# Scattering the second layer's expert results by choice and token, and joining the weighted sum to the expert stage

## The chip, the cores and the metric

The kernel runs on one core of a Trainium2 chip. The metric is the device time of one execution in microseconds (us). The trace numbers every time from the start of its own span. The engines are TensorE (PE; its weight loads are PEld), VectorE (DVE), ScalarE (ACT), GpSimd (POOL) and SyncE (SP), each with its own queue of instructions; SPq, ACTq and POOLq are the queues' DMA issues.

## What is computed

A decoder of two layers over 2048 tokens of width 256, in float32. Each layer adds an attention and a mixture of experts to the residual x. The change concerns the second layer's experts:

```python
N = T * K                    # 2048 tokens, 4 choices each, 32 experts
C = 2 * N // E               # capacity of an expert: 512 rows
scores = softmax(x @ gate_w.T); topk_w, topk_ids = top_k(scores, K); topk_w /= topk_w.sum(-1)
order = argsort(flat_ids); tok = order // K
pos = arange(N) - starts[sorted_eid]
buf = zeros((E, C, 256)).at[sorted_eid, pos].set(x[tok], mode='drop')
g, u = split(einsum('ech,ehf->ecf', buf, w13)); eo = einsum('eci,eih->ech', silu(g) * u, w2)
out_slots = eo[sorted_eid, pos]          # beyond the capacity this reads the expert's last row
routed = zeros_like(x).at[tok].add(out_slots * flat_w[order][:, None])
out = residual + routed + shared
```

The first layer's experts have no capacity.

## The kernel before, in words

The program is a row of blocks, with all engines meeting between them: `norm_block0`, `route_block` 0, `attention_block0` over batches 0 and 1 ("scatter"), `expert_block` 0, `attention_block0` over batches 2 and 3 ("combine"), `norm_block1`, `route_block` 1, `attention_block1`, `expert_block` 1, `combine_block1`. Each block has one instruction stream for each engine, written by hand, with semaphores between them; `wait_ge` stops the engine that carries it and all that is queued behind.

Routing gives each pair of token and choice a slot in `xs`, a table in device memory of 96 tiles of 128 rows; each expert owns whole tiles. `tile_expert` says which expert a tile belongs to. `xs` is filled with zeros at the start (12 DMAs of 1 MB), then GpSimd scatters the normalised rows of `s.xn` there, one indirect DMA for one token tile and one choice (`scatter_tile`, line 761). In the second layer 24 of these 64 run in `route_block` 1, which begins with the first only when VectorE has written the slots (lines 743 and 744), and 40 in `attention_block1`.

`expert_block` works through 95 tiles. SyncE loads a tile of `xs` into one of four buffers (line 1185). TensorE turns it with two transposes (line 1209), multiplies it with the gate and up weights (line 1219), turns the hidden values (line 1228) and multiplies them with the down weights (line 1237). VectorE copies the turned rows (line 1291), makes the product of gate and up (line 1297) and copies the turned hidden values (line 1303). ScalarE does the silu (line 1264) and copies the result into one of four buffers (line 1271), and issues its store to `ys` (line 1273). In step i TensorE does tile i's two gate/up products with tile i+2's transposes between, then turns tile i-1's hidden values, then multiplies tile i-2's with the down weights (first layer: i-8's).

`combine_block1` follows the barrier. GpSimd gathers the 64 tiles of 128 rows (16 token tiles, 4 choices) from `ys` by slot (line 1708); VectorE adds each to x with its weight (line 1720), four for a tile, each waiting for the one before; SyncE stores two token tiles of x together (line 1701). A pair beyond the capacity has the slot of the expert's last row for this gather and an index out of range for the scatter.

In `attention_block0` ScalarE and GpSimd split the query weights of a head into a high and a low part (lines 1101, 856), SyncE loads `wq` and `khT` for each head (lines 837, 841), and GpSimd also makes the keys and sums the rotated query (lines 867, 872).

## Time and profile before

| | us |
|---|---|
| median of 3 timed runs | 1323.95 (1322.92 to 1324.11) |
| profiled execution | 1324.33 |
| its span in the trace | 1323.1 |
| PE busy | 1102.8 (83%) |
| DVE busy | 780.4 (59%) |
| ACT busy | 522.8 (40%) |
| POOL busy | 510.3 (39%) |

The busy times are sums over the whole span, through stages that have different limits. The mean granted TensorE clock is 0.92 of full speed. DMA moved 167.21 MB.

### The profile page before, as it was taken

How to read it: one execution, taken by the hardware profiler on the slowest of the kernel's cores; microseconds unless marked ns; L12 is line 12 of the kernel's file. 1: busy time of each engine (PE TensorE's matmuls, PEld its weight loads, DVE VectorE, ACT ScalarE, POOL GpSimd, SP SyncE). 2: the span in 40 equal slices, each digit the busy share in tenths (PEclk: the TensorE clock that was granted, in tenths of full speed). 3: DMA queues.
4: the chain of work that ended last, by engine and by line, in shares of the span. 5: the costliest groups of instructions: out<-in, count | busy, mean ns of one | idle time of the engine just before them, and what ended most of it. 6: DMA issues, size and time to landing. Idle time of an engine off the chain costs nothing. (4 is left out here: it accounts for less than half of the span.)

```text
span 1323.1 us, 19843 instructions
## 1 busy us (share of the span) xinstructions
PE 1102.8 (83%) x5538; PEld 827.4 (63%) x5538; DVE 780.4 (59%) x1925; ACT 522.8 (40%) x1419; POOL 510.3 (39%) x487
## 2 busy tenths in 40 slices
PE   5659999999969999688889999959679979999100
PEld 5436667777859998355557777855357658888100
DVE  5868776666115554599997776257337545545233
ACT  2336765555204444355555555031123324444000
POOL 0657776565000000565565564033634300000575
PEclk9879999999979999699999999979969979999655
DMA  9432222221455654422222221035579235554343
GB/s 359 186 100 84 89 93 80 76 72 53 191 143 175 182 180 156 109 75 76 77 72 72 77 72 32 1 84 230 184 223 273 101 93 163 162 162 156 99 130 112
DMA packets 116998, 167.21 MB, mean 126 GB/s; under 512 B 15248, under 2 KB 88848, under 8 KB 114832
## 3 DMA queue, kind: packets, MB, share of 16 engines
q1 hardware_dynamic: 77248, 107.46, 26.3%
q0 software_dynamic: 12288, 33.57, 8.0%
q10 hardware_dynamic: 27360, 24.92, 5.4%
q8 instruction: 52, 0.85, 0.3%
q14 instruction: 50, 0.41, 0.1%
HBM read 103.11 MB, written 62.78 MB: 125 GB/s over the span
## 5 line engine op out<-in xcount | busy, mean ns | idle before, releaser
L1219 PE MATMUL bank<-big_a,probsT 128*128 x760 | 201.8, 361 | 0.1
L856 POOL TENSOR_TENSOR parts<-wq,parts 128x256 fp32r<-128x256 f32 x64 | 48.9, 764 | 382.6 <-ACT parts L1101 382.6
L1110 ACT ACTIVATE probs<-bank,negmax 128x256 f32<-128x256 f32 (+3 forms) x256 | 135.0, 537 | 121.4 <-DVE negmax L1025 112.8
L917 PE MATMUL bank<-kT,qT 128*128 128x256 f32 (+3 forms) x512 | 171.7, 457 | 0.0
L933 PE MATMUL bank<-const,probs 128*128 128x128 f32 x640 | 129.6, 275 | 26.8 <-DVE probs L1037 26.7
L949 PE MATMUL bank<-probsT,big_b 128*128 128x512 f32 (+3 forms) x512 | 149.1, 434 | 0.0
L1219 PEld LDWEIGHTS bank<-big_a,probsT 128*128 128x128 f32 x760 | 131.6, 196 | 20.8 <-issue 2.2
L1025 DVE TENSOR_REDUCE negmax<-bank 128x1 f32<-128x256 f32 (+3 forms) x256 | 113.6, 486 | 47.4 <-PE bank L919 46.2
L1297 DVE TENSOR_TENSOR work<-work,bank 128x96 f32<-128x96 f32 (+1 forms) x190 | 51.6, 271 | 151.5 <-ACT work L1264 151.4
L1708 POOL DMA_INDIRECT big_a<-ys_dram,slot_r x64 | 62.4, 975 | 200.2 <-PEq L1691 181.0
L901 PE MATMUL bank<-parts 128*128 128x512 f32 x256 | 116.9, 492 | 20.3 <-POOL parts L856 15.3
L1123 ACT ACTIVATE probsT<-bank,kh 128x512 f32<-128x512 f32 (+3 forms) x256 | 118.5, 528 | 20.7 <-PE bank L933 20.0
L949 PEld LDWEIGHTS bank<-probsT,big_b 128*128 128x128 f32 x512 | 86.0, 190 | 51.2 <-issue 23.4
L1209 PE MATMUL bank<-const,probs 128*128 128x128 f32 x380 | 105.8, 281 | 14.0 <-DMA probs<-xs_dram 13.9
L955 PE MATMUL bank<-big_b,big_a 128*128 128x256 f32 x512 | 116.3, 379 | 0.0
L1037 DVE TENSOR_SCALAR probs<-probs,rsum 128x512 f32<-128x512 f32 (+3 forms) x256 | 114.8, 512 | 2.3
L917 PEld LDWEIGHTS bank<-kT,qT 128*128 128x128 f32 x512 | 83.3, 193 | 47.3 <-issue 36.2
L933 PEld LDWEIGHTS bank<-const,probs 128*128 128x128 f32 x640 | 83.9, 141 | 44.5 <-DVE probs L1037 31.3
L955 PEld LDWEIGHTS bank<-big_b,big_a 128*128 128x128 f32 x512 | 96.8, 190 | 12.7
L1271 ACT ACTIVATE work<-bank 128x256 f32<-128x256 f32 x190 | 73.0, 384 | 71.7 <-PE bank L1237 71.0
L1264 ACT ACTIVATE work<-bank 128x96 f32<-128x96 f32 (+1 forms) x190 | 50.3, 264 | 122.5 <-PE bank L1219 122.5
L761 POOL DMA_INDIRECT xs_dram<-xn,slot_w x64 | 63.3, 990 | 75.3 <-DVE shift L1630 45.0
(210 smaller groups left out, 2023.3 us busy)
## 6 DMA issues: line engine op xcount, KB each, us to landing
probs<-xs_dram SPq DMA_DIRECT2D x190, 128.0 KB
ys_dram<-work ACTq DMA_DIRECT2D x190, 128.0 KB
work<-khT_dram SPq DMA_DIRECT2D x64, 256.0 KB
xs_dram<-big_a SPq DMA_DIRECT2D x12, 1024.0 KB, 20.0
wq<-in_wq SPq DMA_DIRECT2D x64, 128.0 KB
big_a<-in_gu SPq DMA_DIRECT2D x1, 6144.0 KB, 18.2
stack_dram<-parts SPq DMA_DIRECT2D x24, 256.0 KB
xlow<-stack_dram SPq DMA_DIRECT2D x48, 128.0 KB
```

Of the source, the lines that this page charges most:

```text
L901: mm = nc.tensor.matmul(s.ps[6][:, :], w_parts[wp][:, u % 2, k, :], (x_high, x_low)[xp][bi][:, k, :], start=n == 0, stop=last)
L917: nc.tensor.matmul(s.ps[bank][:, at:at + w], s.qT[:, par, i * P:(i + 1) * P], s.kT[:, par, 0:w], start=True, stop=False)
L933: mm = nc.tensor.transpose(s.ps[bank][:, at + (i - j) * P:at + (i - j + 1) * P], s.probs[:, par, ROW_AT[i] + j * P:ROW_AT[i] + (j + 1) * P ...
L949: mm = nc.tensor.matmul(s.ps[7][:, j * P:], s.vp[:, rows[u // H0] * ROWS + j, :], s.probsT[:, COL_AT[j]:COL_AT[j] + w], start=n == 0, stop ...
L955: mm = nc.tensor.matmul(s.ps[bank][:, 0:EMB], s.oT[bi][:, h, i * P:(i + 1) * P], s.wout[:, h, :], start=h == 0, stop=h == H0 - 1)
L1025: v.tensor_reduce(s.negmax[:, par, i:i + 1], s.ps[bank][:, at:at + (i + 1) * P], AX.X, ALU.max, negate=True).then_inc(maxed, 1)
L1037: v.tensor_scalar(row, row, s.rsum[:, par, i:i + 1], None, ALU.mult).then_inc(prob_ready, 1)
L1110: nc.scalar.activation(s.probs[:, par, ROW_AT[i]:ROW_AT[i] + (i + 1) * P], s.ps[bank][:, at:at + (i + 1) * P], ACT.Exp, bias=s.negmax[:, p ...
L1123: nc.scalar.activation(s.probsT[:, COL_AT[j]:COL_AT[j] + w], s.ps[bank][:, at:at + w], ACT.Copy, scale=s.kh[:, rows[bi] * ROWS + j, H0 + h ...
L1209: mm = nc.tensor.transpose(s.ps[i % 2][:, k * P:(k + 1) * P], rows_in[:, i % UNROLL, k * P:(k + 1) * P], s.c("ident"))
L1219: mm = nc.tensor.matmul(s.ps[2 + i % 2][:, 0:W], rowsT[:, i % 2, k * P:(k + 1) * P], gu[:, k, bass.ds(e * W, W)], start=k == 0, stop=k == ...
L1271: nc.scalar.activation(outs[:, j], s.ps[6 + i % 2][:, 0:EMB], ACT.Copy).then_inc(out_ready, 1)
```

## The change

The result of a tile no longer goes to `ys` by slot. Each row of `xs` is 264 columns wide instead of 256 and carries, behind the 256 values, the numbers of the token's four experts (offset by layer) and four destinations, one for each choice: row 512 + token + 2048 x choice of a new table `yk`. While a tile is in the second layer's expert stage, VectorE compares its rows' four expert numbers with the tile's expert (`meet`) and so finds each row's destination (`place`; a row without one goes to the first 512 rows, which are not read). GpSimd scatters the result tile to `yk` by these. `yk` from row 512 on is filled with zeros by 16 DMAs of 512 KB during the first attention. When all scatters have landed SyncE loads the four planes (choices) of two token tiles at a time with plain DMAs, and VectorE adds them with their weights, two tiles in alternation.

Pairs beyond the capacity have no row in `xs`. Their weight is zero in the new `kept_weight`; GpSimd sums their weights by token and expert at the start of `attention_block1` (eight operations), row 127 of each result tile is stored to `last` by SyncE, one gather fetches each expert's last row, and TensorE multiplies the two into PSUM, which VectorE adds. All of this is in `expert_block` 1; `combine_block1` and its barrier are gone. The first layer's expert stage stays, but for the wider rows.

```diff
+XW = EMB + 2 * TOPK
+TRASH = UNROLL * P
+PLACES = 8
+ZEROS = 16
...
norm_block0, SyncE:
+            sp.dma_start(s.xn[:, :, DEST_AT:XW], d["dest"].rearrange("p (t k) -> p t k", t=TILES)).then_inc(dest_in, 16)
-            for c in range(12):
-                sp.dma_start(xs[:, 2048 * c:2048 * (c + 1)], zeros).then_inc(xs_zeroed, 16)
+            for c in range(ZEROS):
+                sp.dma_start(xs[:, ZERO_W * c:ZERO_W * (c + 1)], zeros).then_inc(xs_zeroed, 16)
...
route_block, GpSimd and VectorE:
+                pool.wait_ge(tagged, 1)
...
+            v.tensor_scalar(s.xn[:, :, EXPERT_AT:DEST_AT], argf[:, :, 0:TOPK], float(1 + EXPERTS * layer), None,
+                            ALU.add).then_inc(tagged, 1)
...
-                link(v.tensor_copy(s.slot_w[:], slots))
-                v.tensor_scalar(s.slot_r[:], s.slot_w[:], OUT_OF_RANGE - 1, None, ALU.bitwise_and).then_inc(slots_done, 1)
+                v.tensor_copy(s.slot_w[:], slots).then_inc(slots_done, 1)
+                kept = kept_weight(s)
+                v.scalar_tensor_tensor(out=kept[:], in0=slot_f.rearrange("p (k t) -> p t k", k=TOPK),
+                                       scalar=float(OUT_OF_RANGE), in1=s.weight[:], op0=ALU.is_lt, op1=ALU.mult)
             dve.wait_ge(row_done, 1)
-            v.tensor_copy(s.tile_expert[:], TILE_ROW[:, :]).then_inc(row_read, 1)
+            if layer == 1:
...
+                v.scalar_tensor_tensor(out=offset_of, in0=ENDS[0:EXPERTS, 0:EXPERTS], scalar=0.0,
+                                       in1=s.c("ident")[0:EXPERTS, 0:EXPERTS], op0=ALU.add, op1=ALU.mult,
+                                       accum_out=s.place_f[0:EXPERTS, 0:1]).then_inc(place_found, 1)
...
+                link(v.tensor_scalar(s.tile_tag[:], TILE_ROW[:, :], float(1 + EXPERTS), None, ALU.add))
+            v.tensor_copy(s.tile_expert[:], TILE_ROW[0:1, :]).then_inc(row_read, 1)
...
attention_block0, SyncE and GpSimd:
+                if extra == "scatter" and u < H0:
+                    if u == 0:
+                        sp.wait_ge(zero_made, 1)
+                    at = u * zeros.shape[1]
+                    sp.dma_start(planes[:, at:at + zeros.shape[1]], zeros).then_inc(zeroed, 16)
...
+                nc.gpsimd.memset(zeros, 0.0).then_inc(zero_made, 1)
...
attention_block1, SyncE (ahead of the weight loads) and GpSimd (ahead of its scatters):
+            sp.wait_ge(dropped, 2 * TOPK)
...
+            for k in range(TOPK):
+                w = s.weight[:, :, k].unsqueeze(2).to_broadcast([P, TILES, EXPERTS])
+                link(nc.gpsimd.tensor_tensor(part if k else s.logits[:], route_scratch(s, k), w, ALU.mult))
+                if k:
+                    link(nc.gpsimd.tensor_tensor(s.logits[:], s.logits[:], part, ALU.add))
+            link(nc.gpsimd.tensor_tensor(s.logits[:], s.logits[:], full, ALU.mult))
...
expert_block, second layer; SyncE:
+                sp.wait_ge(out_ready, i + 1)
+                sp.dma_start(d["last"][i:i + 1, :], outs[P - 1:P, i % UNROLL]).then_inc(last_out[i % UNROLL], 16)
...
                     sp.wait_ge(turned, i - UNROLL + 1)
+                    if layer == 1:
+                        sp.wait_ge(met, i - UNROLL + 1)
...
+                if layer == 1 and i >= LAST_LAG:
+                    last_row(i - LAST_LAG)
...
GpSimd:
+                for i in range(N):
+                    j = i % UNROLL
+                    pool.wait_ge(placed, i + 1)
+                    pool.wait_ge(out_ready, i + 1)
+                    if i >= IN_FLIGHT:
+                        ago = i - IN_FLIGHT
+                        pool.wait_ge(y_out[ago % UNROLL], 16 * (ago // UNROLL + 1))
+                    nc.gpsimd.indirect_dma_start(
+                        out=d["yk"], out_offset=bass.IndirectOffsetOnAxis(ap=s.place[:, i % PLACES:i % PLACES + 1], axis=0),
+                        in_=outs[:, j], in_offset=None,
+                    ).then_inc(y_out[j], 16)
+                total.gpsimd(pool)
...
ScalarE:
                     act.wait_ge(y_out[j], 16 * (i // UNROLL))
+                    if layer == 1:
+                        act.wait_ge(last_out[j], 16 * (i // UNROLL))
                 nc.scalar.activation(outs[:, j], s.ps[6 + i % 2][:, 0:EMB], ACT.Copy).then_inc(out_ready, 1)
-                act.wait_ge(out_ready, i + 1)
-                act.dma_start(d["ys"][i * P:(i + 1) * P, :], outs[:, j]).then_inc(y_out[j], 16)
+                if layer == 0:
+                    act.wait_ge(out_ready, i + 1)
+                    act.dma_start(d["ys"][i * P:(i + 1) * P, :], outs[:, j]).then_inc(y_out[j], 16)
...
VectorE:
+            def meet(i):
+                row = rows_in[:, i % UNROLL]
...
+                v.scalar_tensor_tensor(out=matched[:, i % 2], in0=row[:, EXPERT_AT:DEST_AT], scalar=s.tile_tag[:, i:i + 1],
+                                       in1=row[:, DEST_AT:XW], op0=ALU.is_equal, op1=ALU.mult,
+                                       accum_out=s.place_f[:, i % UNROLL:i % UNROLL + 1]).then_inc(met, 1)
+            def place(i):
...
+                v.tensor_tensor(s.place[:, i % PLACES:i % PLACES + 1], s.place_f[:, i % UNROLL:i % UNROLL + 1],
+                                s.c("trash")[:, i % UNROLL:i % UNROLL + 1], ALU.max).then_inc(placed, 1)
...
             for i in range(N + 2):
                 if i < N:
                     hidden(i)
+                if layer == 1 and i + 2 < N:
+                    meet(i + 2)
                 if i + 2 < N:
                     rowsT_out(i + 2)
+                    if layer == 1:
+                        place(i + 2)
                 if 1 <= i < N + 1:
                     hidT_out(i - 1)
...
+def combine1(nc, s, d, sem, out_ready, y_out, last_out, landed):
...
+    def sync(sp):
+        yk = d["yk"][TRASH:, :].rearrange("(k t p) e -> p k t e", k=TOPK, t=TILES)
+        for j in range(UNROLL):
+            sp.wait_ge(y_out[j], landed[j])
+        for g in range(PAIRS):
+            for k in range(TOPK):
+                sp.dma_start(planes[:, k, 2 * g:2 * g + 2], yk[:, k, 2 * g:2 * g + 2]).then_inc(plane_in[g], 16)
...
+    def vector(dve):
+        for g in range(PAIRS):
+            dve.wait_ge(plane_in[g], 16 * TOPK)
+            for k in range(TOPK):
+                for i in range(2):
+                    t = 2 * g + i
                     if k:
-                        dve.wait_ge(x_added, TOPK * t + k)
+                        dve.wait_ge(x_added, ADDS * g + 2 * (k - 1) + i + 1)
+                    v.scalar_tensor_tensor(out=s.x[:, t, :], in0=planes[:, k, t], scalar=weight[:, t, k:k + 1],
+                                           in1=s.x[:, t, :], op0=ALU.mult, op1=ALU.add).then_inc(x_added, 1)
+            dve.wait_ge(summed, g + 1)
+            dve.wait_ge(x_added, ADDS * g + 2 * TOPK)
+            v.tensor_tensor(s.x[:, 2 * g:2 * g + 2, :], s.x[:, 2 * g:2 * g + 2, :],
+                            s.ps[DROPPED_BANKS[g]][:, :].rearrange("p (t e) -> p t e", t=2), ALU.add).then_inc(x_added, 1)
...
```

In `combine1` TensorE also turns the 16 tiles of dropped weights into PSUM, ScalarE copies them out (four copies), GpSimd gathers the last rows, TensorE does 16 products of 32 x 128 by 256, and ScalarE issues the eight stores of x.

## Rows read from the trace of the kernel before

**Rows 1.** Busy time by stretch: us, then PE, PEld, DVE, ACT, POOL (count), clock, DMA.
```profile
1075.00:1225.00 150.00, 150.00 (x828) 126.47 (x827) 75.30 (x276) 60.40 (x183) 0.00 (x0) 1.00 0.51 157
1235.00:1323.10 88.10, 0.00 (x0) 0.00 (x0) 31.02 (x64) 0.00 (x0) 61.39 (x63) 0.50 0.40 119
```
**Rows 2.** The chain that ended last, its end: start us, us, what.
```profile
1317.40 0.49 DVE x_res L1720
...
1318.96 0.48 DVE x_res L1720
```
**Rows 3.** Groups from 1235 us on: form, count, busy us, mean ns, idle before.
```profile
L1708 POOL DMA_INDIRECT big_a<-ys_dram,slot_r x63 | 61.4, 974 | 19.2 <-issue 19.2
L1720 DVE SCALAR_TENSOR_TENSOR x_res<-big_a,weight,x_res 128x256 f32<-128x256 f32 x64 | 31.0, 485 | 59.5 <-DMA big_a<-ys_dram,slot_r 57.8
```
**Rows 4.** Timeline, one period of the second expert loop: start us, us, engine, line.
```profile
1122.02 0.27 PE L1228 MATMUL bank<-const,work 128*128 128x128 f32 x1
...
1122.42 0.29 DVE L1297 TENSOR_TENSOR work<-work,bank 128x128 f32<-128x128 f32 x1 [0.81 <-ACT work L1264]
...
1122.62 0.42 DVE L1291 COPY probsT<-bank 128x256 f32<-128x256 f32 x1
...
1122.96 0.28 DVE L1303 COPY work<-bank 128x128 f32<-128x128 f32 x1
...
1123.65 0.27 PE L1228 MATMUL bank<-const,work 128*128 128x128 f32 x1
1123.65 0.30 PEld L1237 LDWEIGHTS bank<-big_b,work 128*128 128x128 f32 x2
```
**Rows 5.** Timeline of ScalarE at the expert loop's end.
```profile
1228.11 0.38 ACT L1271 ACTIVATE work<-bank 128x256 f32<-128x256 f32 x1 [0.27 <-PE bank L1237]
...
1230.08 0.38 ACT L1271 ACTIVATE work<-bank 128x256 f32<-128x256 f32 x1 [0.46 <-PE bank L1237]
```
**Rows 6.** One scatter of GpSimd, and the landing of all 128 of line 761.
```profile
922.70 0.98 POOL L761 DMA_INDIRECT xs_dram<-xn,slot_w  x1 [0.30 <-issue]
...
DMA to landing us min/median/max: 2.4/2.4/3.4
```
**Rows 7.** One DMA issue on SyncE, among many of a row.
```profile
904.55 0.43 SPq L433 DMA_DIRECT2D stack_dram<-parts  x1
```
**Rows 8.** DMA in the stretch from 2 to 10 us, the opening loads.
```profile
DMA packets 2427, 2.60 MB, mean 325 GB/s; under 512 B 82, under 2 KB 2297, under 8 KB 2427
```
**Rows 9.** Timeline of VectorE: such operations in a row, sixteen and two.
```profile
870.95 6.42 DVE L1409 SCALAR_TENSOR_TENSOR xn<-big_a,kh,probs 128x256 f32<-128x256 f32 x16
...
918.90 1.28 DVE L670 TENSOR_TENSOR x_res<-x_res,bank 128x512 f32<-128x512 f32 x2
```
**Rows 10.** Timeline of VectorE: a one-column operation and its successor.
```profile
906.95 0.15 DVE L724 TENSOR_SCALAR big_a<-big_a 128x1 f32<-128x1 f32 x1
907.02 0.68 DVE L730 SCALAR_TENSOR_TENSOR big_a<-bank,big_a 128x512 f32<-128x512 f32 x1
```
**Rows 11.** Group of the readings of an accumulated sum, on ScalarE.
```profile
L1110 ACT ACTIVATION_READ_ACCUMULATOR probs<-bank,negmax 128x1 f32 x256 | 53.6, 209 | 0.0
```
**Rows 12.** The first attention's start: a stretch before it, then its timeline.
```profile
50.00:60.00 10.00, 6.60 (x36) 4.49 (x37) 8.22 (x13) 0.00 (x0) 9.45 (x8) 0.56 0.00 0
...
73.30 0.42 ACT L1101 ACTIVATE parts<-wq 128x256 fp32r<-128x256 f32 x1 [1.62 <-DMA wq<-in_wq]
75.75 0.42 ACT L1101 ACTIVATE parts<-wq 128x256 fp32r<-128x256 f32 x1 [2.03 <-DMA wq<-in_wq]
...
79.79 0.77 PE L901 MATMUL bank<-parts 128*128 128x512 f32 x1 [2.28 <-DVE work L300]
```
**Rows 13.** GpSimd: a group of 512-column operations; its first instruction in the second attention.
```profile
L872 POOL TENSOR_TENSOR qT<-work 128x512 f32<-128x512 f32 x64 | 83.8, 1309 | 2.7 <-DVE work L300 2.7
...
970.81 0.99 POOL L761 DMA_INDIRECT xs_dram<-xn,slot_w  x1 [17.58 <-DVE shift L1630]
```
**Rows 14.** GpSimd's first scatter in the second routing.
```profile
914.75 1.03 POOL L761 DMA_INDIRECT xs_dram<-xn,slot_w  x1 [8.02 <-DVE slot_r L744]
```

More of the change, by code:

```diff
@@ L53 @@
 PROJ0 = PGATE0 + EXPERTS
-_CONST = dict(ident=P, before=P, upto=P, ones=P, mask=P, iota=EXPERTS, index=1,
+_CONST = dict(ident=P, before=P, upto=P, ones=P, mask=P, iota=EXPERTS, index=1, trash=UNROLL,
               cos0=SEQ, sin0=SEQ)
@@ L113, in make_buffers @@
     s.tile_expert = sb("tile_expert", [1, SLOT_TILES], I32)
+    s.tile_tag = sb("tile_tag", [P, SLOT_TILES])
+    s.place = sb("place", [P, PLACES], I32)
+    s.place_f = sb("place_f", [P, UNROLL])
+    s.last_tile = sb("last_tile", [P, 1], I32)
     s.logits = sb("logits", [P, TILES, EXPERTS])
@@ L384, in route_block @@
     RANK, small = s.ps[0], s.ps[1]
[L385 removed]
+    COUNT, ENDS, TILE_ROW = small[0:EXPERTS, 0:P], small[:, P:P + 2 * EXPERTS], small[:, 2 * P:2 * P + SLOT_TILES]
     if layer == 0:
@@ L827, in attention_block0 @@
         gu_in, stat, aggr = map(sem, ("gu_in", "stat", "aggr"))
+        zero_made, zeroed = sem("zero_made"), sem("zeroed")
+        zeros = s.big_a[:, 0:TOPK * TOKENS * EMB // (P * H0)]
+        planes = d["yk"][TRASH:, :].rearrange("(p r) e -> p (r e)", p=P)
         block = ctx.enter_context(nc.Block())
@@ L1176, in expert_block, with last_row @@
         y_out = [sem(f"y_out{j}") for j in range(UNROLL)]
+        last_out = [sem(f"last_out{j}") for j in range(UNROLL)]
+        met, placed = sem("met"), sem("placed")
+        N = USED_TILES
+        landed = [16 * len(range(j, N, UNROLL)) for j in range(UNROLL)]
+        total = combine1(nc, s, d, sem, out_ready, y_out, last_out, landed) if layer == 1 else None
         block = ctx.enter_context(nc.Block())
-        N = USED_TILES
         @block.sync
         def _(sp):
+            def last_row(i):
+                sp.wait_ge(out_ready, i + 1)
+                sp.dma_start(d["last"][i:i + 1, :], outs[P - 1:P, i % UNROLL]).then_inc(last_out[i % UNROLL], 16)
             for i in range(N):
@@ L1190, in _ @@
                         sp.dma_start(dn[:, at:at + w], d["dn0"][:, at:at + w]).then_inc(w_in, 16)
+                if layer == 1 and i >= LAST_LAG:
+                    last_row(i - LAST_LAG)
+            if layer == 1:
+                for i in range(N - LAST_LAG, N):
+                    last_row(i)
+                total.sync(sp)
             if DOWN_CHUNKS:
                 sp.wait_ge(w_in, 16 * DOWN_CHUNKS)
+        if layer == 1:
+            @block.gpsimd
+            def _(pool):
+                for i in range(N):
[10 more added lines that the diff above has]
+                total.gpsimd(pool)
         @block.tensor
@@ L1256, in _ @@
                     down(i - LAG)
+            if layer == 1:
+                total.tensor(pe)
         @block.scalar
@@ L1279, in _ @@
                     out(i - LAG)
-            for j in range(UNROLL):
-                act.wait_ge(y_out[j], 16 * len(range(j, N, UNROLL)))
+            if layer == 0:
+                for j in range(UNROLL):
+                    act.wait_ge(y_out[j], landed[j])
+            else:
+                total.scalar(act)
         @block.vector
@@ L1408, in _ @@
                 dve.wait_ge(xn_ready, t + 1)
-                v.scalar_tensor_tensor(out=s.xn[:, t, :], in0=xn1[:, t, :], scalar=rms[:, t:t + 1], in1=nw,
+                v.scalar_tensor_tensor(out=s.xn[:, t, 0:EMB], in0=xn1[:, t, :], scalar=rms[:, t:t + 1], in1=nw,
                                        op0=ALU.mult, op1=ALU.mult).then_inc(xf_ready, 1)
@@ L1514, in _ @@
         def _(pool):
+            link = Link(pool, dropped)
+            full, part = route_scratch(s, 9), route_scratch(s, TOPK)
+            for k in range(TOPK):
[4 more added lines that the diff above has]
+            link(nc.gpsimd.tensor_tensor(s.logits[:], s.logits[:], full, ALU.mult))
             late = [(t, k) for t in range(EARLY_TILES, TILES) for k in range(TOPK)]
@@ L1842 @@
          for name, a in arrays.items()}
-    for name, shape in dict(khT=(H0, TOKENS), stack1=(BATCH, 3, P, 2, SEQ), xs=(SLOTS, EMB), ys=(USED_TILES * P, EMB)).items():
+    for name, shape in dict(khT=(H0, TOKENS), stack1=(BATCH, 3, P, 2, SEQ), xs=(SLOTS, XW), ys=(USED_TILES * P, EMB),
+                             yk=(TRASH + TOPK * TOKENS, EMB), last=(USED_TILES, EMB)).items():
         d[name] = nc.dram_tensor(f"{name}_dram", shape, mybir.dt.float32).ap()
```

133 lines of the change are left out of this document (93 added, 40 removed).

## The prediction

> **What bounds the kernel now.** I read three things in this order. First the busy time by stretch [rows 1]: in the second layer's expert stage TensorE is busy 150.00 of 150 us at full clock, and from 1235 us on it does nothing, for 88 us up to the end of the span at 1323.1. Then the chain that ended last [rows 2] and the costliest groups of that stretch [rows 3]: the end is a relay of gathers. GpSimd issues 64 indirect DMAs of 974 ns with 19.2 / 63 = 0.30 us between them; four of them feed one tile's four additions, VectorE works 31.0 us and sits idle 59.5 us. So the end is set by GpSimd's issue rate, not by VectorE or by bytes (119 GB/s, DMA share 0.40 [rows 1]). Last, one period of the expert loop [rows 4], since the change puts work there: TensorE turns a tile's hidden values at 1122.02 and the next tile's at 1123.65, a period of 1.63 us that it fills; every other engine waits for it.
>
> **The end of the kernel, as it becomes.** The time of the last tile's copy does not move unless the loop slows (below): it ends at 1230.08 + 0.38 = 1230.46 [rows 5]. From there to the end of the span it is 92.6 us now. The new path:
>
> 1. Scatters. GpSimd needs 0.98 + 0.30 = 1.28 us for each indirect DMA [rows 6], and the last copies come closer than that: the third last and the last are ready at 1228.49 and 1230.46 [rows 5]. The three scatters start near 1228.6, 1229.9 and 1231.2; the last is issued by 1232.2. A scatter lands 2.4 us (at most 3.4) after its issue [rows 6]; I take 2.6: 1234.8.
> 2. Loads of the planes. SyncE was only waiting; 32 DMAs at about 0.43 us each [rows 7] are 14 us of issue, ahead of the data. They carry 8.39 MB in 1 KB runs. The nearest row for plain loads in 1 KB runs is the opening load of x: queue 1 moved 2.60 MB at 325 GB/s in the first 10 us [rows 8]. One pair of tiles is 1.05 MB, 3.2 us, after some 2.2 us of issue and latency (close to the 2.4 of a 128 KB scatter [rows 6]): the first pair is there at 1234.8 + 2.2 + 3.2 = 1240.2. With the 0.26 MB of output of a pair the pitch by bytes is 1.31 / 0.325 = 4.0 us.
> 3. The sums. A pair has eight scalar_tensor_tensor of 256 columns and one addition of 512 columns from PSUM. The same form without a wait on its predecessor takes 6.42 / 16 = 0.40 us of pitch [rows 9]; in the present end it is 0.52 (1317.40 to 1318.96 is three [rows 2]) as each waits for the one directly before. The new order alternates two tiles, so the wait is for the one before last: I take 0.40. The addition is 1.28 / 2 = 0.64 [rows 9] plus 0.1 for its wait: 8 x 0.40 + 0.74 = 3.9 us a pair. Bytes (4.0) and VectorE (3.9) are level: 1240.2 + 7 x 4.0 + 3.9 = 1272.1.
> 4. The last store: from VectorE's end (1318.96 + 0.48 = 1319.44 [rows 2]) to the span's end is 3.66 us now, and the same after: 1275.8.
>
> So the span shrinks by 47.3 us. Both bounds of the end: 0.52 for all 64 additions gives 8 x 4.9 = 39.2, 7.3 us more; and 250 GB/s, between 325 and the 157 GB/s that the expert stage moves at half the share [rows 1], gives 5.2 us a pair, 10 us more. Below: if 380 GB/s held and VectorE alone set the pitch, 1.2 us less. The correction for dropped rows (16 turns and 16 small matmuls on an idle TensorE, four ScalarE copies of about 0.6 us, one gather of 1 + 2.8 us) is first wanted after the first pair's eight additions, at about 1243.4; the gather can start behind the last scatter at 1232.2 and is in by 1236. Hidden; if that cover were gone it would cost its 4 us once.
>
> **The expert loop.** Removed: ScalarE's store issue of 0.33 us, which nobody waited for. Added on GpSimd: 1.28 us a tile in a period of 1.63, with up to three in flight. Queued behind GpSimd's waits is nothing but the next scatter; ScalarE waits for the scatter of four tiles earlier before it overwrites its buffer, 6.5 us later, against 0.1 + 1.0 + 2.6 = 3.7 us of round trip. SyncE now waits for the tile's row 127 between two loads; that moves a load by about 1.2 us (a down product, the copy of 0.38, an issue of 0.43 [rows 5, 7]), and a load is issued four periods (6.5 us) ahead of its use and needs about 2.4. Bytes: loads grow by 3% to 1056 B a row, the stores change queue; the share was 0.51 [rows 1].
>
> VectorE is where it could bind. Between its product L1297 and its copy L1303 come three small instructions, two for the match (the operation and the reading of its sum) and one for the place. What they must not exceed: the copy of the turned hidden ends at 1122.96 + 0.28 = 1123.24 and TensorE loads it at 1123.65 [rows 4]; less 0.05 for the semaphore that is a slack of 0.36 us. An instruction on one column holds the engine for 0.07 us when the next need not wait for it (L724 at 906.95, L730 at 907.02 [rows 10]). The reading of a sum isn't shown on VectorE; the lower bound is 0, the nearest row is ScalarE's, 209 ns [rows 11]. I take 0.07 + 0.12 + 0.07 = 0.26 us: it fits, cost nil. The upper bound has every one run to its end, 0.15 + 0.21 + 0.15 = 0.51: an excess of 0.15, and since the path from one tile's gate product to the next but one spans two periods, half of it a tile, 0.075 x 95 = 7 us. The waits themselves are satisfied early; L1297 to L1291 is 0.20 us for 128 columns with such waits between [rows 4].
>
> The copies in this loop let their successor start before they end (L1291 at 1122.62 for 0.42, L1303 at 1122.96 [rows 4]). The Trainium skill, "VectorE: DVE Perf Modes", section "The DRAIN you can't avoid", says that the next operation does not start until the pipe is empty, which its section on two Vector instructions with no wait between them limits to held ones; the latter also says that an operation with an accumulator output is two instructions. By the first rule the cost would be that of the second rival; the trace speaks for the second section, and on the two instructions no run here shows it yet.
>
> **Everything earlier.** (a) Rows of 264 columns: 12.98 instead of 12.58 MB of zeros, 1 us more of a transfer that is over before 50 us, from where the DMA engines stand still for 10 us; the first attention splits its first weights only at 73.30 [rows 12]. The destinations arrive as 2048 pieces of 16 B, whose price no row shows; the same gap covers them. Cost 0, up to 3. (b) In the first attention 8.39 MB of zeros on SyncE's queue, one 512 KB piece a head (1.6 us at 325 GB/s). Behind the first stands head 1's wq load: used at 75.75, it would come at about 77.8, its low part at 78.9, while TensorE takes head 1's query at 79.79, released by VectorE [rows 12]; the key product behind it on GpSimd ends 1 us later. I take 0.5 us. The memset of 1024 columns before split_low is at most two operations of 512 columns, 2.6 us [rows 13]; GpSimd is first wanted when ScalarE's first split ends, and that takes a load of about 2.4 us and 0.42 from the block's start, to 73.72 [rows 12]: hidden. (c) Second routing: one 64-column operation more and one less ahead of GpSimd's first scatter at 914.75, which waits on L744 [rows 14]: -0.1. Four small ones before the tile row delay the next batch's products by 1 us, but GpSimd turns to that batch only behind eight scatters, 8 x 1.28 = 10 us after 914.75. (d) Second attention: eight GpSimd operations of 512 columns at 1.3 us, with their waits some 1.4, are 11 us from the block's start at 957.2, up to 968.6; GpSimd's first scatter is at 970.81 after 17.58 us of idle time [rows 13]. The weight loads queued behind SyncE's new wait start 5 us later and are wanted at 1069. Hidden; if not, at most 1.
>
> **Sum.** 1323.1 - 47.3 + 0.5 - 0.1 = 1276.2 of span; the profiled execution took 1324.33, so 1.2 more: 1277.4. The three timed runs have their median at 1323.95, 0.4 below the profiled one; with 1 us for the small things of (a) and (c) I say 1278.
>
> **Rivals.**
> - *VectorE becomes the loop's bound.* The three small instructions exceed 0.36 us. For it: the accumulator's price isn't shown, ScalarE's is 0.21. Against: VectorE is idle 0.8 us of each period (L1297 [rows 4]). Price 1 to 7 us: 1279 to 1285, with the doubled stall of both neighbours up to 1290. Chance 0.2.
> - *The end runs slower than its parts.* Reads at 250 GB/s or additions at 0.52: 1285 to 1288. For it: 157 GB/s at half share would be 310 at full. Chance 0.14.
> - *The scatter's round trip paces the loop (slower than before).* Three may be in flight, and each waits for the landing of the third before it; the place is GpSimd's wait at the head of each scatter. It decides from a round trip of 3 x 1.63 = 4.9 us, and eats the whole gain at 3 x (1.63 + 46/95) = 6.3; at 7 us the period is 2.33 and the time 1278 + 67 = 1345. Against: 2.4 to 3.4 us to landing, plus 1 of issue [rows 6]. Chance 0.04.
> - *The change does not do what it says.* The sums join the stage but the planes are loaded only after the last landing, so nothing overlaps the experts; if the loads then went at the present end's 119 GB/s, 10.5 MB would take 88 us and the time stay within 0.2% of before, 1323. Against: those 119 GB/s are GpSimd's pitch. Chance 0.02.
>
> **How the numbers follow.** Likeliest (0.6): 1278, within 1272 to 1284. The range reaches over the first two rivals, 1271 to 1290, and leaves out the last two and the far ends. A measurement of this kernel can tell about 0.2% (2.6 us) from no change. Faster 0.95, same 0.01, slower 0.04.
>
> **What would show it.** Right: L1297's period 1.63 us still; 95 scatters of about 1 us on GpSimd; some 10 us between the last copy and the first sum; nine VectorE operations a pair in about 4 us; the span ending 45 us after the last copy. Wrong: TensorE idle before its load of the turned hidden, released by VectorE's L1303 counterpart (first rival); VectorE waiting long for planes (second); ScalarE's copy waiting for the scatter (third); a late start of the first attention, before 80 us.

## The result, and the profile after

| | before | after |
|---|---|---|
| median of the timed executions | 1323.53 | 1278.97 (1260.3 to 1281.7, 4) |
| profiled execution | 1324.33 | 1279.91 |
| its span | 1323.1 | 1278.1 |
| DMA moved, MB | 167.21 | 177.53 |

The ratio is 0.959, with a 95% interval of 0.948 to 0.970. It is taken over the executions within 1.5% of the fastest of their kernel only, and since one of the four read 1260.3 those are two, 1260.3 and 1278.03; that is also why the interval is wide. Times the 1323.95 of the front table it gives 1269.5, under the forecast range of 1271 to 1290, while the median, 1278.97, stands 1 us above the forecast 1278. On two further chips the changed kernel gave 0.968 [0.966, 0.970] and 0.970 [0.969, 0.971], 1281.4 and 1284.2 by the same reckoning, and no second execution near 1260. In medians the time fell by 44.6, 41.5 and 38.9 us on the three chips.

The 45.0 us between the two spans, cut at the first instruction of ScalarE in each stage and at the end of its last copy in the expert loop:

| stage | before | after | difference |
|---|---|---|---|
| start to first attention | 0 to 70.62 | 0 to 74.10 | +3.5 |
| first attention to start of second attention | 70.62 to 957.06 | 74.10 to 960.36 | -0.2 |
| second attention | to 1069.66 | to 1069.83 | -3.1 |
| second expert loop, to last copy's end | to 1230.46 | to 1231.73 | +1.1 |
| last copy to end of span | 92.6 | 46.4 | -46.3 |

The kernel after, busy time by stretch, in the columns of [rows 1] (us, then PE, PEld, DVE, ACT, POOL with counts, clock, DMA share, GB/s); the first line answers to the first of [rows 1], the others lie in the new end:

```profile
1075.00:1225.00 150.00, 149.89 (x821) 125.51 (x820) 94.43 (x547) 59.59 (x181) 84.76 (x89) 0.99 0.54 160
1236.00:1278.00 42.00, 13.99 (x32) 10.46 (x32) 30.92 (x72) 0.00 (x0) 0.00 (x0) 0.51 0.77 251
1242.00:1250.00 8.00, 8.00 (x20) 6.28 (x19) 7.11 (x17) 0.00 (x0) 0.00 (x0) 0.50 1.07 337
1250.00:1260.00 10.00, 1.18 (x3) 0.36 (x2) 9.69 (x24) 0.00 (x0) 0.00 (x0) 0.50 1.09 367
```

TensorE still fills the expert loop. In the end VectorE is busy for the same 31 us as in [rows 3] (26.0 us of weighted additions and the eight additions from PSUM), now almost without gaps (9.69 of 10 us), and the DMA engines run at 337 to 367 GB/s instead of 119.

The groups of that end (form, count, busy us, mean ns, idle before) show the same, beside [rows 3]:

```profile
L1889 DVE SCALAR_TENSOR_TENSOR x_res<-big_a,slot_r,x_res 128x256 f32<-128x256 f32 x64 | 26.0, 478 | 12.3 <-DMA big_a<-yk_dram 12.3
L1876 PE MATMUL bank<-big_b 32*128 32x256 f32 x32 | 14.0, 633 | 4.1 <-issue 4.1
```

VectorE waits for planes once, 12.3 us, for the first; before it waited for gathers 57.8 us. The second line is the correction for the dropped rows, on TensorE at its lower clock (0.50, 1.2 GHz), beside the additions.

The timeline of the kernel after, from the last scatters to the end (start us, us, engine line op, [idle before <-releaser]):

```profile
1229.43 0.96 POOL L1275 DMA_INDIRECT yk_dram<-work,place  x1 [0.60 <-issue]
1230.84 0.96 POOL L1275 DMA_INDIRECT yk_dram<-work,place  x1 [0.44 <-DMA yk_dram<-work,place]
1232.30 0.96 POOL L1275 DMA_INDIRECT yk_dram<-work,place  x1 [0.50 <-DMA yk_dram<-work,place]
1233.57 0.96 POOL L1275 DMA_INDIRECT yk_dram<-work,place  x1 [0.30 <-DMA last_dram<-work]
...
1242.79 3.25 DVE L1889 SCALAR_TENSOR_TENSOR x_res<-big_a,slot_r,x_res 128x256 f32<-128x256 f32 x8 [12.31 <-DMA big_a<-yk_dram]
1246.15 0.69 DVE L1893 TENSOR_TENSOR x_res<-x_res,bank 128x512 f32<-128x512 f32 x1
1246.75 3.25 DVE L1889 SCALAR_TENSOR_TENSOR x_res<-big_a,slot_r,x_res 128x256 f32<-128x256 f32 x8
...
1274.21 0.69 DVE L1893 TENSOR_TENSOR x_res<-x_res,bank 128x512 f32<-128x512 f32 x1 [0.46 <-DVE x_res L1889]
```

Last copy 1231.73, last scatter 1233.57, first sum 1242.79, then one pair of tiles each 3.96 us, last sum done 1274.90, end 1278.1.

One period of the expert loop in the kernel after, to be laid beside [rows 4]:

```profile
1151.01 0.29 DVE L1392 TENSOR_TENSOR work<-work,bank 128x128 f32<-128x128 f32 x1 [0.60 <-ACT work L1353]
1151.22 0.22 DVE L1406 SCALAR_TENSOR_TENSOR wq<-probs,tile_tag 128x4 f32<-128x4 f32 x1
1151.36 0.08 DVE L1406 DVE_READ_ACCUMULATOR wq<-probs,tile_tag 128x1 f32 x1
1151.36 0.42 DVE L1386 COPY probsT<-bank 128x256 f32<-128x256 f32 x1
1151.70 0.15 DVE L1415 TENSOR_TENSOR place<-place_f,const 128x1 int32<-128x1 f32 x1
1151.76 0.28 DVE L1398 COPY work<-bank 128x128 f32<-128x128 f32 x1
1152.24 0.30 PEld L1324 LDWEIGHTS bank<-big_b,work 128*128 128x128 f32 x2
1152.64 0.29 DVE L1392 TENSOR_TENSOR work<-work,bank 128x128 f32<-128x128 f32 x1 [0.59 <-ACT work L1353]
```

The period is 1152.64 - 1151.01 = 1.63 us, as before. The match and the reading of its sum hold VectorE for 1151.36 - 1151.22 = 0.14 us, the place for 0.06. The copy of the turned hidden values ends at 1152.04, 0.20 us before TensorE loads them (line 1324); before the change it was 0.41.

### The profile page after: what moved, and what is told of

It is laid out like the page before. It is cut to its first block and busy times, and to the rows that moved or that the text cites. A ratio compares the mean times of both kernels' runs of the same rounds, so it can differ in the third digit from the quotient of the medians.

```text
span 1278.1 us, 20689 instructions
## 1 busy us (share of the span) xinstructions
PE 1119.2 (88%) x5586; PEld 839.3 (66%) x5586; DVE 801.9 (63%) x2224; ACT 524.2 (41%) x1423; POOL 548.8 (43%) x528
## 2 busy tenths in 40 slices
DMA packets 118684, 177.53 MB, mean 139 GB/s; under 512 B 17231, under 2 KB 86958, under 8 KB 118046
## 5 line engine op out<-in xcount | busy, mean ns | idle before, releaser
L1078 DVE TENSOR_REDUCE negmax<-bank 128x1 f32<-128x256 f32 (+3 forms) x256 | 113.6, 485 | 47.2 <-PE bank L972 46.1
L1275 POOL DMA_INDIRECT yk_dram<-work,place x95 | 91.1, 959 | 90.4 <-DVE place L1415 53.6
```

The lines of the kernel that those rows point to most:

```text
L1078: v.tensor_reduce(s.negmax[:, par, i:i + 1], s.ps[bank][:, at:at + (i + 1) * P], AX.X, ALU.max, negate=True).then_inc(maxed, 1)
L1275: nc.gpsimd.indirect_dma_start(out=d["yk"], out_offset=bass.IndirectOffsetOnAxis(ap=s.place[:, i % PLACES:i % PLACES + 1], axis=0), in_=ou ...
```

## The experiments

Each kernel ran beside the kernel before on its chip: the first four on one chip (before 1325.05), the next four on a second (1324.11), the last three on a third (1325.88). Spans are of the profiled execution.

**The changed kernel again.** No edit.

> The changed kernel unchanged, to see how its own time spreads. Its first executions took 1278 to 1282 us and once 1260. Theory A: one of its stages has two ways to run and the 1260 comes again in a share of the executions, so the times fall in two groups near 1260 and 1280. Theory B: that one was an outlier, and all stand within 0.3% of 1279.

Measured: 1283.53 (1279.5 to 1284.17), ratio 0.968 [0.966, 0.970], span 1282.2. Neither expectation holds: the 1260.3 did not come back, and four of the five executions lie more than 0.3% above 1279. From the last copy to the end it was 47.2 us in this profile, 46.4 in the first and 46.8 in the third chip's; the larger part of the difference in time lies ahead of that.

**The destinations' load moved from the start to the first routing.**

```diff
 norm_block0, SyncE:
-            sp.dma_start(s.xn[:, :, DEST_AT:XW], d["dest"]...).then_inc(dest_in, 16)
...
 route_block 0, SyncE, at its start:
+                sp.dma_start(s.xn[:, :, DEST_AT:XW], d["dest"]...).then_inc(tagged, 16)
```

> The load of the destinations (2048 pieces of 16 B) is moved from the first block, where SyncE was held 6.75 us by its issue ahead of the sixteen zero transfers, into the first routing block, where SyncE is idle. Theory: the first block ends when SyncE has issued the last of the zeros, 3.5 us later than before the change, so this gives 3.5 us back and the first attention starts near 70.6 instead of 74.1. Rival: the longer zero transfers and not the issue delay the first attention; then nothing changes.

Measured: 1280.4 (1275.38 to 1283.48), ratio 0.965 [0.963, 0.968]. The intervals of the two kernels overlap, so the times alone do not show the gain; the profiles do. Timeline of the unchanged kernel's second execution, SyncE's issues, then ScalarE's first instruction in the first routing stage and in the first attention (start us, us, what):

```profile
6.65 6.62 SPq L213 DMA_DIRECT2D xn<-in_dest  x1
13.31 23.98 SPq L218 DMA_DIRECT2D xs_dram<-big_a  x16
...
38.32 1.28 ACT L511 ACT_TABLE_LOAD   x1 [4.34 <-PEq L169]
...
73.49 1.06 ACT L1147 ACTIVATE parts<-xnT 128x1024 fp32r<-128x1024 f32 x1 [4.05 <-PEq L169]
```

The same of the kernel with the load moved:

```profile
6.50 21.45 SPq L217 DMA_DIRECT2D xs_dram<-big_a  x16
36.40 0.65 SPq L460 DMA_DIRECT2D xn<-in_dest  x1
36.40 1.28 ACT L511 ACT_TABLE_LOAD   x1 [1.34 <-PEq L169]
...
70.36 1.06 ACT L1147 ACTIVATE parts<-xnT 128x1024 fp32r<-128x1024 f32 x1 [4.06 <-PEq L169]
```

The first attention starts 3.1 us earlier, at about the time of the kernel before (70.62): that is nearly all of the +3.5 in the table. What delays it is not the transfer but its issue. Behind the opening loads the 2048 pieces of 16 B hold SyncE for 6.6 us, and the zeros behind them end at 37.3, with the load moved at 28.0, before the change at 24.4; VectorE's last copy of that stage is done at 34.5 in the unchanged kernel. The barrier of the stage waits for SyncE: in all eight profiles with the load at the start the next stage begins 1.0 to 1.1 us after SyncE's last zero issue, in the five others 0.8 us after VectorE's last copy. Of the 3.1 us, 1.9 are gained at that barrier (38.32 to 36.40, with VectorE itself 1.1 us later than in the unchanged kernel), the other 1.2 in the routing stage behind it, whose length varies from 34.0 to 35.4 us over the profiles. Issued into an idle queue the same load holds SyncE for 0.65 us. The Trainium skill, "DMA: Bandwidth & Descriptors", section "Anatomy of one DMA — SWDGE (gpsimd) path", calls the making of descriptors small and says that many can be emitted before their cost shows; it speaks of GpSimd's path, not of SyncE's. The 0.65 us fits that. The 6.6 us does not, and differs from it only in what was queued ahead; that the queue was full is a reading that no run shows.

**Two scatters in flight instead of three.**

```diff
-    LAST_LAG, IN_FLIGHT = 7, 3
+    LAST_LAG, IN_FLIGHT = 7, 2
```

> Only two scatters may be in flight instead of three. Theory of the round trip: each scatter waits for the landing of the second before it, issue 0.96 plus 2.4 to landing plus about 0.5 for the two waits is 3.9 us, halved 1.93 us a tile instead of 1.63, 95 x 0.30 = 29 us more, 1308. Rival: the landing is not what GpSimd waits for; then the time stays at 1279.

Measured: 1305.93, 22 us more than the kernel unchanged beside it. That is under the expected 29: the first twenty tiles still run at 1.63 us, and only then does the period become some 1.86 us, a round trip of 3.7. From first silu to last the loop takes 171.1 us against 154.1, and its last copies and the end add 3.6. Waits of this kernel in the loop (who waited for what: us in total, times, longest):

```profile
ACT work L1362 <- DMA yk_dram<-work,place: 58.0, 53, 3.0
DVE work L1392 <- ACT work L1353: 50.6, 87, 2.3
POOL yk_dram L1275 <- ACT work L1362: 50.2, 56, 1.9
```

So the third rival's mechanism is real: ScalarE's copy waits for a scatter to land, VectorE for ScalarE, TensorE behind them. Its point lies at 3.3 us of round trip with two in flight, and was 4.9 with three; 3.7 is between the two, which is why it costs nothing in the change.

**Six more one-column operations a tile on VectorE, and then two.** The result is not read.

```diff
                 v.tensor_tensor(s.place[:, ...], s.place_f[:, ...], s.c("trash")[:, ...], ALU.max).then_inc(placed, 1)
+                for n in range(6):          # second kernel: range(2)
+                    v.tensor_tensor(spare[:, at:at + 1], s.place_f[:, ...], s.c("trash")[:, ...], ALU.max)
```

> Six more one-column operations on VectorE per tile, right behind the place and ahead of the copy of the turned hidden values. The three added by the change took 0.20 us together and left 0.15 us of slack after the semaphore. Theory: six at 0.06 are 0.36 us, 0.21 over the slack, half of that per tile, so 95 x 0.105 = 10 us more, 1289. Rival 1: the excess counts in full, 20 us more. Rival 2: TensorE's order hides it, no change.

Measured: 1299.28 (1294.65 to 1299.84), 15.7 us more, midway between the theory's 10 and the first rival's 20. VectorE in that kernel's loop:

```profile
1150.65 0.15 DVE L1415 TENSOR_TENSOR place<-place_f,const 128x1 int32<-128x1 f32 x1
1150.72 0.51 DVE L1420 TENSOR_TENSOR wq<-place_f,const 128x1 f32<-128x1 f32 x6
1151.14 0.29 DVE L1398 COPY work<-bank 128x128 f32<-128x128 f32 x1
...
1151.56 0.30 PEld L1324 LDWEIGHTS bank<-big_b,work 128*128 128x128 f32 x2 [0.16 <-issue]
```

Each holds VectorE for 0.42 / 6 = 0.07 us, as [rows 10] said. The expectation had the slack wrong. It allowed 0.05 us from the copy's end to TensorE's load, but 81 of 82 such loads in this kernel's loop follow the copy by 0.13 or 0.14 us (above: 1151.43 to 1151.56), and in no profile does one follow sooner. So the 0.20 us of the changed kernel hold 0.07 us of slack, not 0.15. 0.42 - 0.07 = 0.35 us of excess, half of it a tile, is 0.175 x 95 = 16.6 us; the loop is 16.0 us longer (170.1 against 154.1), where the full excess would be 33. The halving of the prediction's first rival is right.

> Two more one-column operations of VectorE in each tile of the second layer's expert loop, which nobody reads. They hold VectorE for 0.07 us each, 0.14 us, against the slack of 0.15 to 0.20 us that the changed kernel's loop shows between VectorE's copy of the turned hidden values and TensorE's load of them. Theory: the period stays 1.63 us and the time that of c1_after_again within 3 us; TensorE's load of the turned hidden follows the copy within 0.1 us. Rival (VectorE binds already, or a semaphore's delay eats the rest): half of 0.14 a tile, 0.07 x 95 = 7 us more.

Measured: 1287.02 (1282.04 to 1291.07), beside 1286.95 for the unchanged kernel. In the medians nothing; in the traces the loop, from its first silu to its last, takes 157.49 us against 153.84, 0.04 us a tile. The expectation of no cost holds within its 3 us in the times and is missed by 0.7 us in the profile; TensorE's load follows the copy by 0.14 us (1151.42 to 1151.56), not within 0.1, and 82 of 89 loads do so by 0.13 or 0.14. That is the same hand-over of 0.13 us: 0.14 - 0.07 = 0.07 us of excess, half a tile, is an estimate of 3.3 us, against 3.7 in the trace. The timeline's slack never reads less than 0.13, so that is where it is used up.

Its unchanged companion:

> The changed kernel as it is, on the same chip as the next two runs. Earlier its executions read 1278 to 1284 us, with a ratio of 0.968. Theory (the steps of the sum hold, the spread comes from when TensorE's granted clock rises in the late stages): 0.966 to 0.970 again, last ScalarE copy to end of span 46.4 us. Rival (the 0.959 of its first measurement is its normal state): 0.959.

Measured: 1286.95 (1284.79 to 1287.72), ratio 0.970 [0.969, 0.971], span 1285.3; last copy to end 46.8 us.

**The kernel before, its gathers and sums put into the expert stage without a barrier.** Gathers, their order and the stores unchanged; GpSimd waits for the landing of all stores of `ys` instead.

```diff
-def combine_block1(nc, s, d):
+def combine1(nc, s, d, sem, out_ready, y_out, landed):
...
+        pool.wait_ge(out_ready, USED_TILES)
+        for j in range(UNROLL):
+            pool.wait_ge(y_out[j], landed[j])
```

> The kernel before with one part of the change alone: its gathers by slot and its sums moved into the second expert stage, without the barrier; ys, slots and the relay of 64 gathers stay. Theory: the barrier is worth only the time between the landing of the last result (about 1232.6) and GpSimd's start at 1233.9, 1 to 2 us, so 1322 to 1323 and a ratio of 0.999; the gain of 44 us is all in what replaces the gathers. Rival: leaving the barrier is a good part of the gain, 5 us or more.

Measured: 1324.45 (1323.52 to 1327.39) against 1324.11. In its trace 91.0 us lie between the last copy (1234.57) and the end (1325.6), 1.6 less than before, and the first gather starts 2.6 us after that copy instead of 3.5. The barrier was worth 1 to 2 us, less than a measurement tells; of the gain of 46 us the other 44 or more come from scatters beside the experts and plain loads after them, which no run takes apart.

**The additions in the old order, four to one tile, then four to the next.**

```diff
-            for k in range(TOPK):
-                for i in range(2):
+            for i in range(2):
+                for k in range(TOPK):
...
-                        dve.wait_ge(x_added, ADDS * g + 2 * (k - 1) + i + 1)
+                        dve.wait_ge(x_added, ADDS * g + TOPK * i + k)
```

> The changed kernel with its additions in the old order, tile by tile, each waiting for the one directly before. Theory: 0.52 us instead of 0.40 for each of 64 additions, 4.9 us a pair instead of 3.95, 7.5 us more at the end. Rival: bytes set the pitch, so that the slower VectorE costs under 3 us.

Measured: 1292.51; last copy to end 52.5 us against 46.4, so +6.1 (its expert stage began late, at 1076.33, which the total contains). VectorE near its end:

```profile
1277.62 4.00 DVE L1889 SCALAR_TENSOR_TENSOR x_res<-big_a,slot_r,x_res 128x256 f32<-128x256 f32 x8
1281.73 0.69 DVE L1893 TENSOR_TENSOR x_res<-x_res,bank 128x512 f32<-128x512 f32 x1
1282.33 4.00 DVE L1889 SCALAR_TENSOR_TENSOR x_res<-big_a,slot_r,x_res 128x256 f32<-128x256 f32 x8
```

A pair takes 4.71 us instead of 3.96, eight additions 4.00 instead of 3.25. Six of the eight wait for the one directly before (the first of each tile does not), so such a wait costs 0.75 / 6 = 0.12 us, the 0.52 for 0.40 that [rows 2] and [rows 9] gave; the 7.5 us expected counted it for all eight. 8 x 0.75 = 6.0 us is nearly the whole difference. VectorE sets the end's pitch.

**Half the sum.** Choices 2 and 3 are left out of the additions; all planes are still loaded.

```diff
-            for k in range(TOPK):
+            for k in range(2):
                 for i in range(2):
```

> The changed kernel with choices 2 and 3 left out of the sum (their planes are still loaded). VectorE needs 2.3 us a pair instead of 3.95. Theory: the planes come at a pitch of about 3.3 to 4.0 us a pair, so they become the bound and the end is 5 to 9 us shorter, not the 13 us that VectorE saves. Rival: VectorE alone is the bound, 13 us less.

Measured: 1275.04; last copy to end 40.45 us, 5.9 less. Now VectorE waits for planes before nearly every pair:

```profile
1263.97 1.67 DVE L1889 SCALAR_TENSOR_TENSOR x_res<-big_a,slot_r,x_res 128x256 f32<-128x256 f32 x4 [1.05 <-DMA big_a<-yk_dram]
1265.75 0.69 DVE L1893 TENSOR_TENSOR x_res<-x_res,bank 128x512 f32<-128x512 f32 x1
1267.54 1.67 DVE L1889 SCALAR_TENSOR_TENSOR x_res<-big_a,slot_r,x_res 128x256 f32<-128x256 f32 x4 [1.11 <-DMA big_a<-yk_dram]
```

The pitch is 3.5 us a pair (3.0 for the first two): that is what the planes need. VectorE's 3.96 lies over it by 0.45, so taking away half of its work, 1.6 us a pair, brings only that much for each pair but the last.

**A version faster than both.** The destinations' load late as above, four scatters in flight, and the additions shared: ScalarE applies the weights of choices 1 to 3 in place, VectorE does two weighted additions of 256 columns and four plain ones of 512 a pair.

```diff
+            act.wait_ge(plane_in[g], 16 * TOPK)
+            for k in (1, 2, 3):
+                for t in (2 * g, 2 * g + 1):
+                    nc.scalar.activation(planes[:, k, t], planes[:, k, t], ACT.Copy,
+                                         scale=weight[:, t, k:k + 1]).then_inc(scaled, 1)
...
+            v.tensor_tensor(planes[:, 1, two], planes[:, 1, two], planes[:, 2, two], ALU.add).then_inc(x_added, 1)
```

> A version meant to beat the change: the destinations loaded in the first routing block (3 us), four scatters in flight (0.3 us), and the weights of choices 1 to 3 applied by the idle ScalarE, so that VectorE has two operations of 256 columns and four of 512 a pair, 3.3 us instead of 3.95 (4 us at the end). Theory: 6 to 8 us below the changed kernel. Rival: the planes' bytes hold the end, then only the 3 us of the start remain.

> The version of b4_best1 unchanged (destinations loaded in the first routing stage, four scatters in flight, ScalarE applies the weights of choices 1 to 3, VectorE adds in 512 columns), beside the changed kernel on one chip. Theory: first attention 3 to 4 us earlier, sums 1 to 2 us shorter: 4 to 6 us below c1_after_again. Rival (its 1274 was chance of the chip): within 2 us of it.

Measured: 1274.15 (1272.2 to 1279.0) on the second chip, where the changed kernel did not run, so that its expected 6 to 8 us are not tested there; on the third 1278.11 (1271.09 to 1278.87), ratio to before 0.962 [0.960, 0.964], where the changed kernel took 1286.95: 8.8 us less, more than the 4 to 6 expected. By the two profiles (spans 1277.1 and 1285.3): first attention at 70.42 instead of 74.80, 4.4 us; the loop from ScalarE's first instruction to its last silu 159.35 against 159.52 us, nothing; the rest, last silu to end, 45.0 us (from 1232.13) against 49.3 (from 1235.96), 4.4 us, where 1 to 2 were expected; the stages between lose 0.7. Of VectorE's timeline in this version:

```profile
1268.73 0.68 DVE L1906 TENSOR_TENSOR x_res<-x_res,big_a 128x512 f32<-128x512 f32 x1
1269.45 0.69 DVE L1908 TENSOR_TENSOR x_res<-x_res,big_a 128x512 f32<-128x512 f32 x1
1270.06 0.87 DVE L1897 SCALAR_TENSOR_TENSOR x_res<-big_a,slot_r,x_res 128x256 f32<-128x256 f32 x2
```

A pair now takes 3.3 us between starts in the steady part (1266.74 to 1270.06), under the 3.5 of the planes. It can, as the first pair takes 4.5 us and lets the planes get ahead: the eighth pair starts 24.4 us after the first, with half the sum, where the planes set the pace, 23.8. The two are level. Which part of the version brings how much was not tried one by one, but for the load of the destinations.

## Where the prediction was wrong, and which of its steps held

**The range.** The ratio puts the front table's time at 1269.5, below 1271. The step that failed is the one that set the spread: "A measurement of this kernel can tell about 0.2% (2.6 us) from no change" left no room for an execution some 18 us shorter than its neighbours, and one of four, 1260.3, was that. No profile fell on it, so what was shorter in it, and why, stays open. Its mean granted clock, 0.933, is no higher than that of the other three (0.937 to 0.940), so a faster clock over the whole is not it; the same holds for the 1301.4 of the kernel before (0.917, the others 0.919 to 0.923). In the sum itself the step that failed is the start, put at 0 with up to 3 and measured at +3.5 (below); it makes the time longer and so does not explain the miss.

**The median's 1 us is in part luck.** The start (+3.5), the loop (+1.1) and the end (+1.0) came out 5.6 us above their steps, and the second attention gave back 3.1 that no step had in it.

**The end (-47.3 predicted, -46.3 measured, 46.4 us long instead of 45.3).** Its steps against the rows: last scatter predicted at 1231.2, is at 1233.57. The third last copy ends at 1230.09 instead of 1228.49, 1.6 us; its scatter starts 0.75 us behind it where I took 0.1 (0.74 behind the copies before it as well), 0.6 us; and the next comes 1.46 us later instead of 1.28, behind an earlier scatter's landing (the "<-DMA yk_dram" above), 0.2 us. First sum 1240.2, is 1242.79, 2.6 us: the 2.4 of the scatter, and behind it two errors that nearly cancel. From the start of the last scatter to the first load's issue (1233.57 to 1236.13) it is 2.6 us where I took 3.6, as the 2.4 us to landing [rows 6] count from an issue's start and not, as I took them, from its end; from there to the first sum it is 6.7 us where I took 5.4. Pitch 4.0, is 3.96; VectorE's 0.40 for each weighted addition, from [rows 9], holds. But "bytes and VectorE are level" was mis-sized on the bytes' side: 325 GB/s [rows 8] was the start's figure, in the end the DMA engines move up to 367 and, with VectorE's load halved, a pair takes 3.5 us. The second rival (250 GB/s, or 0.52 for each addition) did not occur; the run in the old order shows what its second half would have cost, 6.1 us.

**The expert loop (0 predicted, +1.1 to +1.8).** The three small instructions hold VectorE for 0.20 us, not 0.26: the reading of a sum is 0.08 us and overlaps, far from the 0.21 of ScalarE [rows 11]. The Trainium skill, "VectorE: DVE Perf Modes", section "Two Vector instructions with no wait between them", says two instructions for an operation with an accumulator output, and both are in the trace, started before their predecessors end (1151.22 before 1151.30, 1151.36 before 1151.44). (The prediction gave the other section's rule the price of the second rival; it meant the 7 us of the first.) The slack was smaller than computed, though: the 0.05 us that the prediction took off for the semaphore stands in no row, and the hand-over takes 0.13 us, so the slack was 0.28 us before the change and is 0.07 after it, not 0.36 and 0.16. From first silu to last the loop takes 153.67 us against 152.28 before and 153.84 and 154.12 in the two further runs: 1.4 to 1.8 us, while the period of most tiles stays 1.63. This is the lower edge of the first rival's 1 to 7 us; which tiles lose it was not traced, but with 0.07 us of slack little is needed.

**The start (0 predicted, up to 3; +3.5 measured).** This is the step of the sum that failed. I asked whether the data of the destinations came in time, and it does; I did not ask what SyncE has queued behind the issue. 6.7 us for the load and four more zero pieces at 1.5 us kept it at work until 37.8, while VectorE's last copy in that stage was done at 34.95, and the barrier passed that on: the next stage begins at 38.79 instead of some 35.8, 3.0 of the 3.5 us. The gap in [rows 12] that was to cover it lies behind the barrier, so it covered the transfer and not the issue. With the load moved the first attention starts 3.1 us earlier.

**Everything else early.** Zeros of `yk` in the first attention: 303.0 us to the stage's end before and after, cost 0 instead of 0.5; but the stage takes 304.4 and 305.2 us in the two further profiles of the changed kernel and 304.1 in the joined version, which has no such zeros, so 0.5 us cannot be told here. GpSimd's eight operations in the second attention: they run at 1.07 to 1.26 us each and end at 970.3, and TensorE's first product there still waits for the sums' load; hidden, as said.

**The second attention (-3.1, not predicted).** Nothing that the change does explains it. Busy time by stretch of the kernel before, in the columns of [rows 1], the granted clock behind POOL's count, here in the second attention:

```profile
975.00:979.00 4.00, 4.00 (x14) 2.86 (x14) 1.75 (x4) 1.28 (x3) 2.87 (x4) 0.50 0.82 234
979.00:983.00 4.00, 4.00 (x19) 2.63 (x17) 1.02 (x2) 0.71 (x2) 0.81 (x1) 0.82 1.04 365
```

The same stretches of the kernel after:

```profile
975.00:979.00 4.00, 4.00 (x20) 3.18 (x20) 2.08 (x6) 1.41 (x3) 3.06 (x4) 0.68 0.61 191
979.00:983.00 4.00, 4.00 (x22) 2.70 (x22) 1.47 (x3) 1.95 (x4) 2.79 (x3) 1.00 0.90 279
```

TensorE begins at 966.5 before and 969.3 after, idle until then, at 0.50 (1.2 GHz). It is granted 1.00 (2.4 GHz) only inside 979 to 983 before, but inside 975 to 979 after. The thirteen profiles fall in two groups. In four, all of the changed kernel or its variants (the first two profiles of it, six more operations, half the sum), the clock rises 8 to 9 us after TensorE's first product, and the stage takes 109.3 to 109.9 us. In the nine others, the kernel before and the third profile of the changed kernel among them, it rises 14 to 15 us after it, and the stage takes 112.4 to 112.8. Some 6 us more at half the clock are the 3 us. The same kernel does both, so it is chance of the execution, and it lets the first measurement look 3 us better than its steps.

The stages between the starts of the two attentions vary by as much: 886.3 us in the first profile of the changed kernel, 889.7 and 889.2 in the next two, 890.1 in the joined version, which runs the code of before there, and 886.4 in the kernel before; so this too is not of the change, and its cause is open. 1278 as the sum of the predicted steps, with +3.5, +1.1 and +1.1 for start, loop and end and less the 0.5 for the zeros, makes 1283. The second median (1283.5) lies there by luck: its profile has 3.3 us more between the attentions and 3.3 less in the second one than the kernel before.

**The rivals in the runs.** VectorE as the loop's bound came out at its lower edge, 1.1 us. The end was not slow. The round trip is real with two scatters in flight and costs nothing with three. The change does what it says: 89 scatters stand in the 150 us of the loop, and the loads behind it run at 337 to 367 GB/s, not at 119.

## What to carry to other kernels

Where a gather by index ends a kernel, see whether the same index can be applied as a scatter while an engine-bound loop still runs: each indirect DMA costs its queue 1.0 + 0.3 us, for free beside a loop of 1.6 us a tile, and the data then comes back by plain loads at about three times the rate (337 to 367 against 119 GB/s). A DMA added ahead of a row of others is to be costed by the issuing queue up to the next barrier, not by when its data is needed. And when work goes into a loop's slack, take off what the hand-over costs: from VectorE's copy to TensorE's load it is 0.13 us here, and the loss begins when the timeline's gap comes down to that.

## What the hardware showed beyond that

- One DMA of 2048 pieces of 16 B held SyncE's issue for 6.62 us behind the opening loads, and for 0.65 us in an idle queue.
- The rise from 0.50 to 1.00 of granted clock in the second attention comes 8 to 9 us or 14 to 15 us after TensorE's first product, in executions of one program, and moves the stage by 3 us.
- From the end of VectorE's copy to TensorE's load of it at least 0.13 us pass, from ScalarE's silu to VectorE's product behind it 0.03 (1150.98 to 1151.01 in the kernel after).
- Rarely an execution is some 20 us shorter than all others of its kernel: 1260.3 of the changed kernel, once in 14; 1301.4 of the kernel before, once in the 7 beside the second group of runs. As both kernels have it, it is not of the change. No profile fell on one, and its cause stays open.
